# A decoder layer with experts: h turned by regrouping DMAs and VectorE, in a loop one block deeper

## The reference

```python
top_vals, top_idx = jax.lax.top_k(logits, 2)          # logits: [2048, 8]
h = silu(einsum('th,ehf->etf', x, w1)) * einsum('th,ehf->etf', x, w3)   # H = 256, F = 1024
out = einsum('etf,efh,te->th', h, w2, w)              # w: two gate values per token
x = layernorm(x + out)
```

## Time and profile before

| | us |
|---|---|
| median of three runs | 701.82 (698.64 to 703.44) |
| span of the profiled execution (its first to its last instruction) | 697.2 |
| blocks in the loop | 36 (L1701 runs 72 times) |
| TensorE busy | 612.1 (88%) |
| VectorE, ScalarE, Pool busy | 404.9, 239.2, 283.3 |

### The profile page before, as it was taken

How to read it: one execution, slowest core, us unless ns; L and a number is a source line. 1 busy time by engine, 2 the same in 40 slices (tenths; PEclk the granted TensorE clock), 3 DMA queues, 4 the chain that set the end, 5 groups by cost and what they waited for, 6 DMA issues and landing times.

```text
span 697.2 us, 13581 instructions
## 1 busy us (share of the span) xinstructions
PE 612.1 (88%) x3780; PEld 482.2 (69%) x3781; DVE 404.9 (58%) x1214; ACT 239.2 (34%) x471; POOL 283.3 (41%) x198
## 2 busy tenths in 40 slices
PE   6999899798798875388999999999999999999940
PEld 2444469586366654367888888888888888888830
DVE  2566588766748879876544545445454454544524
ACT  3555540002876551224223242232422323321204
POOL 7000020012364456566516738167381373751112
PEclk9999999799899887568999999999999999999995
DMA  8999409004000043322431331613325115111117
GB/s 277 328 335 336 126 1 243 1 1 177 5 2 1 32 168 120 113 99 57 169 68 30 105 121 30 211 30 115 111 43 198 30 30 196 30 30 32 31 21 235
DMA packets 54003, 74.78 MB, mean 107 GB/s; under 512 B 13392, under 2 KB 50640, under 8 KB 52688
## 3 DMA queue, kind: packets, MB, share of 16 engines
q1 hardware_dynamic: 42064, 60.58, 26.1%
q0 software_dynamic: 6864, 9.11, 7.5%
q10 hardware_dynamic: 5040, 4.66, 2.5%
HBM read 42.67 MB, written 31.67 MB: 107 GB/s over the span
## 4 chain that ended last, share of the span: by engine, by line
PE 68%; DVE 14%; POOL 5%; ACT 5%; DMA 4%; issue 3%; POOLq 0%; DVEq 0%; SPq 0%; ACTq 0%
PE bank L2197 26%; PE bank L2217 12%; PE bank L1769 7%; PE bank L1928 4%; PE bank L2207 4%; POOL experts_w L817 3%; DVE region L1259 2%; DVE region L1257 2%; DMA region<-slots 1%; PE bank L1819 1%; PE bank L1778 1%; PE bank L2152 1%; DVE small L1276 1%; PE bank L1785 1%; PE bank L2096 1%
## 5 line engine op out<-in xcount | busy, mean ns | idle before, releaser
L2197 PE MATMUL bank<-experts_w,experts_x 128*128 (+1 forms) x864 | 216.1, 399 | 3.6 <-POOL experts_w L817 2.3
L2197 PEld LDWEIGHTS bank<-experts_w,experts_x 128*128 128x128 f32 x864 | 157.0, 188 | 37.1 <-issue 4.4
L1701 DVE TENSOR_TENSOR region<-region,bank 128x512 f32<-128x512 f32 x72 | 49.5, 687 | 159.9 <-ACT region L1083 159.9
L1083 ACT ACTIVATE region<-bank 128x512 f32<-128x512 f32 x72 | 43.0, 597 | 238.5 <-PE bank L2197 238.5
L830 POOL DMA_INDIRECT total<-region,rid x36 | 55.8, 1549 | 165.2 <-DVE region L1715 105.8
L2217 PE MATMUL bank<-experts_w 128*128 (+1 forms) x864 | 120.9, 289 | 1.9 <-DVE experts_w L1705 1.9
L2217 PEld LDWEIGHTS bank<-experts_w 128*128 128x128 f32 x864 | 107.8, 191 | 2.2 <-issue 2.2
L817 POOL TENSOR_TENSOR experts_w<-wstage,experts_w 128x3072 f32 x12 | 83.6, 6964 | 0.5
L698 POOL TENSOR_TENSOR small<-small 128x4 f32<-128x4 f32 (+5 forms) x19 | 25.0, 1320 | 105.4 <-DVE small L1268 86.7
L1769 PE MATMUL bank<-xcol,region 128*128 128x512 f32 x128 | 59.0, 619 | 7.3 <-DMA xcol<-in_xT 5.7
L1155 DVE SCALAR_TENSOR_TENSOR region<-bank,convw,region 128x511 f32<-128x511 f32 (+2 forms) x48 | 35.9, 748 | 34.9 <-ACT region L873 33.0
(11 more groups left out here) (344 smaller groups left out, 878.8 us busy)
## 6 DMA issues: line engine op xcount, KB each, us to landing
wstage<-in_w_exp SPq DMA_DIRECT2D x8, 3072.0 KB, 10.8
slots<-padrow SPq DMA_DIRECT2D x8, 2210.0 KB, 19.3
region<-slots ACTq DMA_DIRECT2D x35, 130.0 KB, 2.1
xcol<-in_xT SPq DMA_DIRECT2D x4, 512.0 KB, 6.7
xtok<-in_x SPq DMA_DIRECT2D x1, 2048.0 KB, 13.3
region<-in_ctxT SPq DMA_DIRECT2D x1, 2048.0 KB, 7.7
region<-in_ctx SPq DMA_DIRECT2D x4, 512.0 KB, 9.6
total<-xtok SPq DMA_DIRECT2D x3, 512.0 KB, 3.2
```

Source lines behind the costliest of these rows:

```text
L1083: act.activation(gsil[:, u], bank[2 * u][:, :], ACT.Silu).then_inc(sil_done, 1)
L1701: dve.tensor_tensor(hmid[:, u], gsil[:, u], bank[2 * u + 1][:, :], ALU.mult).then_inc(mid_done, 1)
L2197: mm = pe.matmul(bank[2 * u + m][:, :], (xTh, xTl)[a][:, s, k, :], moving(off, w, m * KD * F + k * F + u * HALF, HALF), start=(k == 0 and ...
```

## The change

- h no longer goes through TensorE's transpose, save in the last block. `middle` writes its product so that the 32 columns of each group lie by fours; when both halves are there, SyncE issues 16 DMAs (`regroup`), each moving 32 partitions with 1 KB to another group of 32 partitions, into `hgrp`. VectorE then transposes 32x32 squares into the same banks as before (`turn`), 128x512 per half. x is turned by TensorE as before.
- The loop is one block deeper: TensorE's pass is up half 0 of g, rows of g + 1, up half 1 of g, both down halves of g - 2. VectorE turns g - 1 and weighs g - 2; Pool sends g - 2. `hmid` and `hgrp` have two buffers, in `xcol`, `hTh` and `hTl` one. Behind the loop come two more blocks' down matmuls; the last block's product is written once more, to `hend`, and turned by TensorE.
- A block's rows are loaded in two DMAs, x (`xq`) earlier, the four other columns (`xm`) later.
- Weights are loaded and split in two parts, up (4096 columns) and down (2048). The up part may be overwritten when the last up matmuls of the old expert are done, a block before its down part. SyncE looks up in a table after each block's regroup whether a part is due (`load_ahead`).
- `NB` is 48 instead of 42, so the optional part of the loop has 8 passes instead of 5.

```diff
 HALF = F // 2
-NB = (2 * T + 2 * P + E * (P - 1)) // P + 1
-NB += NB % 2
...
@@ -533,28 +544,79 @@
...
-            for n in range(2, E):
-                with sp.If(events > n):
-                    e = sp.value_load(tab_ev[0:1, n:n + 1], min_val=0, max_val=E - 1)
-                    sp.wait_ge(w_ready, n)
-                    sp.dma_start(wstage, w_exp[bass.ds(e, 1)].squeeze(0)).then_inc(w_loaded, 16)
...
+            def regroup(g, s):
+                if not isinstance(g, int) or g >= 2:
+                    sp.wait_ge(turned, 2 * g - 2)
+                    sp.sem_inc(sp_gate, 1)
+                sp.wait_ge(mid_done, 2 * g + 2)
+                for a in range(NC):
+                    for c in range(NC):
+                        sp.dma_start(hgrp[CH * c:CH * (c + 1), s, a], hmid[CH * a:CH * (a + 1), s, c]).then_inc(grouped[s], 16)
...
+            def load_up(e):
+                sp.dma_start(wstage[:, 0:ACT_PART], w_exp[bass.ds(e, 1)].squeeze(0)[:, 0:ACT_PART]).then_inc(w_up_loaded, 16)
...
+            def load_ahead(g):
+                with sp.If(sp.value_load(tab_load[0:1, bass.ds(g - 1, 1)], min_val=0, max_val=1) > 0):
+                    event = event_of(g - 1)
+                    e = expert_of(event + 2)
+                    sp.wait_ge(w_low_up, event)
+                    load_up(e)
+                with sp.If(sp.value_load(tab_load[0:1, bass.ds(g - 2, 1)], min_val=0, max_val=1) > 0):
+                    event = event_of(g - 2)
+                    e = expert_of(event + 2)
+                    sp.wait_ge(w_ready, event + 2)
+                    load_down(e)
+
+            sp.wait_ge(y_sent[1], 16)
+            regroup(0, 0)
+            regroup(1, 1)
+            with sp.If(events > 2):
+                sp.wait_ge(w_ready, 2)
+                load_up(expert_of(2))
+            regroup(2, 0)
+            with sp.If(events > 2):
+                load_down(expert_of(2))
+            load_ahead(2)
+
+            def pair(p):
+                regroup(2 * p - 1, 1)
+                load_ahead(2 * p - 1)
+                regroup(2 * p, 0)
+                load_ahead(2 * p)
+            with sp.Fori(0, SURE - 2) as it:
+                pair(it + 2)
+            with sp.Fori(0, NB // 2 - SURE) as it:
+                with sp.If(npair - it > SURE):
+                    pair(it + SURE)
+
...
-            def next_high(g):
...
+                pool.wait_ge(w_hi, event + 2)
+                pool.sem_inc(pool_gate, 1)
+                pool.tensor_tensor(lo_of(off)[:, 0:ACT_PART], wstage[:, 0:ACT_PART], hi_of(off).bitcast(F32)[:, 0:ACT_PART],
+                                   ALU.subtract).then_inc(w_low_up, 1)
+
+            def split_down(g):
+                event, off = event_of(g), next_off(g)
+                pool.wait_ge(w_low_up, event)
+                pool.wait_ge(w_down_loaded, 16 * event)
+                pool.wait_ge(down_done, 2 * g)
                 pool.sem_inc(pool_gate, 1)
                 pool.tensor_tensor(hi_of(off)[:, ACT_PART:], wstage[:, ACT_PART:], bc(zero[:, 0], 1, [P, WCOLS - ACT_PART]),
                                    ALU.add).then_inc(w_rest, 1)
...
+                pool.wait_ge(w_rest, event)
+                pool.sem_inc(pool_gate, 1)
+                pool.tensor_tensor(lo_of(off)[:, ACT_PART:], wstage[:, ACT_PART:], hi_of(off).bitcast(F32)[:, ACT_PART:],
+                                   ALU.subtract).then_inc(w_ready, 1)
...
             def pair(p):
                 for s in range(2):
                     g = 2 * p + s
...
+                    with pool.If(begins(g)):
+                        low_up(g)
+                    if isinstance(g, int) and g == 1:
+                        continue
+                    send_block(g - 2, s)
+                    with pool.If(begins(g - 1)):
+                        split_down(g - 1)
...
+                if not isinstance(g, int) or g:
+                    act.wait_ge(down_done, 2 * g + (u - 1))
                 act.copy(hTh[:, u], bank[4 + u][:, :].rearrange("p (c t) -> p c t", t=P)).then_inc(hTh_done, 1)
+
+            def high_up(g):
+                with act.If(act.value_load(tab_first[0:1, bass.ds(g, 1)], min_val=0, max_val=1) > 0):
+                    event = act.value_load(tab_event[0:1, bass.ds(g, 1)], min_val=1, max_val=E - 1)
+                    off = act.value_load(tab_noff[0:1, bass.ds(g, 1)], min_val=0, max_val=max(slot_at))
+                    act.wait_ge(up_done, 2 * g)
+                    act.wait_ge(w_up_loaded, 16 * event)
+                    act.sem_inc(act_gate, 1)
+                    act.copy(hi_of(off)[:, 0:ACT_PART], wstage[:, 0:ACT_PART]).then_inc(w_hi, 1)
...
+                    load_rows(g + 2, s)
+                    load_meta(g, s)
+                    if not start:
+                        high_up(g)
+                    silu(g, 0)
                     silu(g, 1)
...
+                    for u in range(2):
+                        high_turned(g - 1, u)
...
-            def middle(g, u):
+            def middle(g, s, u):
                 dve.wait_ge(sil_done, 2 * g + (u + 1))
-                dve.tensor_tensor(hmid[:, u], gsil[:, u], bank[2 * u + 1][:, :], ALU.mult).then_inc(mid_done, 1)
-
-            def low_turned(g, u):
+                by_part = "p (c a r) -> p c a r"
+                dve.tensor_tensor(hmid[:, s, :, 4 * u:4 * u + 4].rearrange("p a c r -> p c a r"),
+                                  gsil[:, u].rearrange(by_part, a=NC, r=CH),
+                                  bank[2 * u + 1][:, :].rearrange(by_part, a=NC, r=CH), ALU.mult).then_inc(mid_done, 1)
...
+            def turn(g, s, u):
+                if u == 0:
+                    dve.wait_ge(grouped[s], 128 * (g - s) + 256)
+                if not isinstance(g, int) or g:
+                    dve.wait_ge(hTl_done, 2 * g + (u - 1))
+                dve.transpose(bank[4 + u][:, :].rearrange("p (c a r) -> p c a r", a=NC, r=CH),
+                              hgrp[:, s, :, 4 * u:4 * u + 4].rearrange("p a c r -> p c a r")).then_inc(turned, 1)
+
...
             def pair(p):
                 for s in range(2):
                     g = 2 * p + s
...
+                    row_meta(g - 1, 1 - s)
+                    middle(g, s, 0)
                     rows(g + 1, 1 - s)
-                    middle(g, 1)
-                    low_turned(g, 0)
-                    if not isinstance(g, int) or g:
-                        weigh(g - 1, 1 - s)
-                    row_meta(g + 1, 1 - s)
+                    middle(g, s, 1)
+                    for u in range(2):
+                        turn(g - 1, 1 - s, u)
+                    for u in range(2):
+                        low_turned(g - 1, u, bank[4 + u], hTh, hTl)
+                    if not isinstance(g, int) or g >= 2:
+                        weigh(g - 2, s)
...
+            for u in range(2):
+                dve.tensor_tensor(hend[:, u], gsil[:, u], bank[2 * u + 1][:, :], ALU.mult).then_inc(mid_done, 1)
+            row_meta(last, 1)
+            for u in range(2):
+                low_turned(last, u, bank[2 * u], endTh, endTl)
+            weigh(last - 1, 0)
             weigh(last, 1)
...
                     pe.wait_ge(w_ready, event + 1)
                     up(g, s, 0, off)
-                    if s == 0:
-                        last_off = offset_of(event_of(g - 1))
-                    turn(g - 1, 1)
-                    down(g - 1, 0, last_off)
                     turn_rows(g + 1, 1 - s)
                     up(g, s, 1, off)
-                    turn(g, 0)
-                    down(g - 1, 1, last_off)
+                    if isinstance(g, int) and g == 1:
+                        continue
+                    off = offset_of(event_of(g - 2))
+                    for u in range(2):
+                        down(g - 2, u, off, hTh, hTl)
...
             last = pe.value_load(tab_n[0:1, 1:2], min_val=2 * SURE - 2, max_val=NB - 2) + 1
+            off = offset_of(event_of(last - 1))
+            down(last - 1, 0, off, hTh, hTl)
+            for u in range(2):
+                last_turn(last, u)
+            down(last - 1, 1, off, hTh, hTl)
             off = offset_of(event_of(last))
-            turn(last, 1)
-            down(last, 0, off)
-            down(last, 1, off)
+            for u in range(2):
+                down(last, u, off, endTh, endTl)
```

More of the change, by code:

```diff
@@ L858, in _ @@
                     pair(it + SURE)
+            last = pool.value_load(tab_n[0:1, 1:2], min_val=2 * SURE - 2, max_val=NB - 2) + 1
+            send_block(last - 1, 0)
+            send_block(last, 1)
             for first, n in ENDS:
@@ L1124, in _ @@
             last = (act.value_load(tab_n[0:1, 1:2], min_val=2 * SURE - 2, max_val=NB - 2) + 1)
-            high_turned(last, 1)
+            for u in range(2):
+                act.wait_ge(turned, 2 * last + (u + 1))
+                act.copy(endTh[:, u], bank[2 * u][:, :].rearrange("p (c t) -> p c t", t=P)).then_inc(hTh_done, 1)
             for u, (first, n) in enumerate(ENDS):
```

(29 more changed lines are left out.)

209 lines of the change are left out of this document (97 added, 112 removed).

## The result

The changed kernel takes 827.91 us (median of 4 runs, 825.09 to 832.37) where the kernel before, measured beside it, takes 702.13 (698.64 to 703.44): a ratio of 1.178, 95% interval 1.174 to 1.181. The profiled execution spans 823.1 us in place of 697.2. Slower was forecast, and by SyncE's issues, but at 717 us with 738 as the upper end; the loss is 126 us and not 15.

The account below looks back on a forecast made before the run. TensorE bounds the kernel before, SyncE's issues the changed one: from 328.5, 35 x 9.13 = 319.6, 21.6 for weights and 23.6 of tail reach 693.3, +15.3 us, so 717 us; range 684 to 738.

Parts of the forecast that it names:

- the rival in which VectorE becomes the bound: VectorE's transposes in the loop set the pace, from 3.0 us per transpose on; 3 in 100, with the slow side.
- the 9.13 us of the sum: SyncE's time per block in the loop, issues plus bookkeeping; 35 blocks gave 319.6 us.
- TensorE's saving: Eight transposes of h leave TensorE per block: 9.56 to 8.76 us, 28.0 us over 35 blocks (25 to 31).
- SyncE's time between the runs: Table reads, branches, waits and loop turn, 2.0 us per block (1.4 to 2.4), plus 21.6 us for weight loads.
- From the last issue's end to the read back: The tail after the last regroup's issue, at 669.7, was put at 23.6 us.
- I take 0.45, nearest to the 0.48, and keep 0.385 to 0.475: Time per SyncE issue behind another in the loop; 16 issues per block then take 7.1 us (6.2 to 7.5).
- the begin of the read back: After the loop's tail, the last send was to land at 693.3; before, the read back began at 678.02.
- The upper bound: Issue pace bounded from above by DMAs in a row: starts 0.48 to 0.51 us apart, or a duration of 0.507.
- the first product: At the loop's start, the first block's product, which starts SyncE's stream, was to be ready at about 328.5.
- up to 1 us per hand-over: Cost of ScalarE's 3.6 us copy before the activation between experts; with 2.3 us of waits saved, put at zero.
- TensorE stays the bound: Rival: SyncE's issues hide in the loop at about 0.385 us each or less, 683 us; chance 0.27.
- The mutual disturbance of SyncE's and ScalarE's issues: ScalarE's row-load issues might hold up SyncE's: up to 0.7 us more per block, +24 us, to 740 us.

Follow-up runs that it names:

- experiment 1: Changed kernel with SyncE issuing 8 of the 16 regroup DMAs per block, half of the turned h stale: 701.7 us, ratio 1.003.
- experiment 4: Kernel before, with nine runs of 16 DMAs on SyncE added behind the loop, varying path, partitions and bytes: 0.63 to 0.64 or 0.46 to 0.48 us between starts.
- experiment 8: Changed kernel with regroup through device memory (ScalarE stores, SyncE issues four loads), weight copy between the silus, old start order: 704.4 us, ratio 1.006.
- experiment 9: Changed kernel with 4 on-chip regroup DMAs per block, row order adapted, weight copy between the silus, old start order: 688.4 us, ratio 0.984.
- experiment 3: Changed kernel without the regroup: TensorE turns h as before; deeper loop, two-part weights and split row loads stay: 715.5 us, ratio 1.021.
- experiment 6: Kernel of experiment 1 with ScalarE's copy of the next expert's weights moved between the two silus: 683.8 us, ratio 0.977 to the kernel before.
- experiment 7: Changed kernel with the 16 regroup DMAs per block shared out, 12 issued by SyncE and 4 by ScalarE: 756.1 us, ratio 1.079.
- experiment 5: Changed kernel with all 16 regroup DMAs moving 256 bytes per partition instead of 1 KB, three quarters of turned h stale: 825.4 us.

## Why the prediction was right and where it failed

*What holds.* That SyncE's issues follow each other without a gap, that TensorE waits in each block for VectorE and VectorE for the regroup, and that no other engine has a part in it, came as forecast (155.6 us of VectorE's 155.7 are for the DMA). The transposes cost 0.706 us (0.7 taken), so the rival in which VectorE becomes the bound had no part; its threshold of 3.0 us each was too high, since 4.6 + 2 x 2.3 already makes the 9.13 us of the sum. TensorE's saving is 0.88 us per block (0.80 taken), seen in experiment 1. SyncE's time between the runs was right: all gaps between the 35 runs of issues sum to 89.5 us in the trace, where 35 x 2.0 + 21.6 = 91.6 were taken. From the last issue's end to the read back it is 24.2 us, against 23.6.

*The step that failed* is the term "I take 0.45, nearest to the 0.48, and keep 0.385 to 0.475", the pace of issues. It measured 0.633. By the starts in the trace the 35 runs of 16 issues sum to 355.3 us, 10.15 each, in place of 35 x 7.13 = 249.6: +105.8 of the 110.9 us by which the begin of the read back was missed (804.23 against 693.3). The reasoning went by the count of pieces per partition, and let a quarter of the partitions shorten an issue, for which it had no row; experiment 4 shows that partitions and bytes change the pace by 0.01 us at most and that two ends on chip add 0.17 us. The upper bound came from rows that all had device memory at one end, so it was no bound for this path. The prediction had itself said that 0.01 us is 5.3 us; 525 x 0.183 is 96; the slower first issue of each run (0.53 on average against 0.38) is 5, and a few stretched ones (up to 1.74 us) are most of the rest.

*A second, smaller miss* is the start: the first product was put at 328.5, and the first regroup went out at 335.2, +6.7. TensorE did not wait 1.5 us for the second block's rows but 4.2: their load was issued at 326.88, not near 321.98, because VectorE's tables came later. The prediction also kept the old start of the first up matmuls, which came 2.0 us later (321.76 against 319.72), and the 24 matmuls behind the wait took 7.38 us where 24 took 5.76 before. Experiments 8 and 9, with the old order there, issue their first store at 328.3 and their first regroup at 327.8, the predicted place. Together: 105.8 - 2.1 + 6.7 + 0.6 = 111.0.

*An error that SyncE's pace covered.* ScalarE's copy ahead of the silu was put at "up to 1 us per hand-over". With TensorE still turning h (experiment 3) that is nearly so, 1.0 to 1.8 us. With the transposes gone and SyncE out of the way it costs 1.8 to 4.6 us at six hand-overs and slow matmuls behind them, 18 us in all (experiments 1 and 6). The rival "TensorE stays the bound" at 683 us was therefore too low for this change with fast issues: experiment 1, which is that case, gives 701.7, and 683.8 comes only with the copy moved. The mutual disturbance of SyncE's and ScalarE's issues, which widened the upper end, is not there: experiment 7 shows the queues at full pace side by side.

*What the change is worth, then.* Moving h off TensorE gains 0.88 us in each of 35 blocks, 31 us. Sixteen issues per block make it a loss of 126 us; with four, and the copy moved, 12 us (1.6%) remain of the 31. From 315 us on TensorE's waits sum to 18.9 us in that version and to 8.6 in the kernel before, mostly at the start, at the hand-overs and in the tail; what makes up the other half of the 19 us was not taken apart. Whether moving the copy alone would change the sixteen-issue kernel was not tried; by its chain, which stays on SyncE, it would not.

## What to carry to other kernels

Price a DMA that is issued in a loop by its path as well as by its count, and take the row from the same path: an estimate whose slope is 5 us per 0.01 us needs a measured term or a range as wide as the ignorance. When issues set the pace, first make them fewer and bigger, which costs nothing here up to 128 partitions of 1 KB, and only then share them out to other queues. Before a bottleneck goes, read what would be late next; the order of one copy and one activation was worth more than half of the gain.

## What the runs showed of the hardware

- An issue on SyncE's queue right behind another costs 0.63 to 0.64 us from on-chip to on-chip memory and 0.46 to 0.48 with device memory at one end, one piece per partition. The first holds for 32, 64 or 128 partitions and for 128 bytes or 1 KB each (experiment 4), for 256 bytes (experiment 5), and for 1 KB pieces from 128 partitions into 4 KB of 32 (experiment 9); the second was measured for 32 and 128 partitions of 1 KB.
- The pace belongs to the queue: SyncE's 12 issues in 7.60 us and ScalarE's 4 in 2.69 overlap (experiment 7).
- A 512 KB store lands in 2.6 us, and in 8.6 to 9.5 when it is issued 0.7 to 1.6 us behind a 2 MB load of another queue (experiment 8).
- After 4.6 us of waiting, TensorE's next 12 matmuls ran at a granted clock of 0.50 and took 5.48 us in place of 3.07 (experiment 1).
